# A selective-scan and expert layer in 512-token chunks: one SiLU in another stretch, paired u products, and two B·u tiles that change engines

## The reference

```python
xn = rmsnorm(layernorm(x), rms_w)
xs, res = split(xn @ W_in, 2)                 # 512 channels each
xs = silu(causal_conv4(xs) + conv_b)
dt, B, C = split(xs @ W_x, [512, 528])        # 16 states
dt = softplus(dt @ W_dt)
h_t = exp(A * dt_t) * h_{t-1} + dt_t * B_t * xs_t     # 512 channels x 16 states
y_t = sum_n h_t[:, n] * C_t[n]
x = x + layernorm(x) + (y * silu(res)) @ W_out
n2 = layernorm(x)
x = x + (silu(n2 @ w1[e]) * (n2 @ w3[e])) @ w2[e]     # expert e has tokens 512e to 512e+511
```

## Time and profile before

| | |
|---|---|
| median of 3 runs | 978.1 us (977.73 to 979.46) |
| the profiled execution, its time | 979.27 us |
| its span | 977.5 us |
| PE, DVE, POOL, ACT busy | 93%, 92%, 91%, 76% of the span |
| granted TensorE clock, mean | 0.982 |

### The profile page before, as it was taken

How to read it: one execution, slowest core, us unless ns; L and a number is a source line. 1 busy time by engine, 2 the same in 40 slices (tenths; PEclk the granted TensorE clock), 3 DMA queues, 4 the chain that set the end, 5 groups by cost and what they waited for, 6 DMA issues and landing times. The chain is left out here.

```text
span 977.5 us, 13189 instructions
## 1 busy us (share of the span) xinstructions
PE 912.5 (93%) x4204; PEld 601.2 (62%) x4204; DVE 900.1 (92%) x1000; ACT 745.8 (76%) x1356; POOL 893.5 (91%) x425
## 2 busy tenths in 40 slices
PE   6989988999999999999999999999999998677988
PEld 4555455655766566755766567655667557554777
DVE  5889899899999999999999999999999989988983
ACT  4577877888779878888879787888788876567771
POOL 1498899999999999999999999999999999998970
PEclk9998999999999999999999999999999999699999
DMA  5580145011651039111471037310580117401100
GB/s 176 227 295 22 43 164 226 1 68 59 259 202 46 23 114 353 54 68 46 182 293 40 29 102 274 144 68 0 188 331 1 47 60 264 153 22 59 52 1 22
DMA packets 43477, 116.82 MB, mean 120 GB/s; under 512 B 8592, under 2 KB 27024, under 8 KB 34192
## 3 DMA queue, kind: packets, MB, share of 16 engines
q1 hardware_dynamic: 41552, 115.94, 31.9%
q10 hardware_dynamic: 1856, 0.04, 0.1%
HBM read 110.21 MB, written 5.77 MB: 119 GB/s over the span
## 5 line engine op out<-in xcount | busy, mean ns | idle before, releaser
L701 DVE TENSOR_TENSOR_SCAN ring<-ebank,state,ring 128x512 f32<-128x512 f32 (+1 forms) x544 | 626.4, 1203 | 36.8 <-ACT ebank L864 28.7
L553 POOL TENSOR_TENSOR hc<-ring,c_all 128x1024 f32<-128x1024 f32 (+1 forms) x256 | 600.4, 2367 | 18.4 <-DVE ring L701 10.7
L864 ACT ACTIVATE ebank<-dt_,a_neg 128x512 f32<-128x512 f32 (+1 forms) x544 | 353.0, 662 | 143.0 <-DVE ring L701 139.5
L1323 PEld LDWEIGHTS ybank<-ident,hc 128*128 128x128 f32 x1920 | 221.0, 142 | 95.4 <-issue 58.0
L542 POOL TENSOR_TENSOR ring<-b_all,u 128x1024 f32<-128x1024 f32 x110 | 261.1, 2374 | 9.9 <-DVE taken L644 9.5
L1323 PE MATMUL ybank<-ident,hc 128*128 128x128 f32 x1920 | 245.2, 276 | 23.0 <-POOL hc L553 14.3
L681 DVE TENSOR_TENSOR ring<-b_all,ubank 128x1024 f32<-128x1024 f32 x144 | 172.0, 1195 | 0.0
L1248 PE MATMUL gbank<-xT,w 128*128 128x512 f32 x280 | 132.0, 603 | 7.1 <-DVE hb L811 6.8
L1248 PE MATMUL gbank<-xT,w_a 128*128 128x512 f32 x256 | 120.1, 606 | 8.0 <-DVE dt_ L669 4.4
L1248 PE MATMUL gbank<-xs,w_a 128*128 128x512 f32 x224 | 100.8, 593 | 0.7 <-ACT sres L896 0.7
L1248 PEld LDWEIGHTS gbank<-xT,w 128*128 128x128 f32 x280 | 50.2, 192 | 64.0 <-issue 46.0
(11 more groups left out here) (164 smaller groups left out, 854.9 us busy)
## 6 DMA issues: line engine op xcount, KB each, us to landing
b_all<-bc_kept SPq DMA_DIRECT2D x32, 1024.0 KB, 6.7
c_all<-bc_kept SPq DMA_DIRECT2D x32, 1024.0 KB, 8.4
w<-in_L_ffn_w_dram SPq DMA_DIRECT2D x16, 640.0 KB, 4.9
w_a<-in_L_attn_W_in_dram SPq DMA_DIRECT2D x7, 1024.0 KB, 4.8
w_a<-wc_kept SPq DMA_DIRECT2D x7, 1024.0 KB, 4.9
w2s<-in_L_ffn_w_dram SPq DMA_DIRECT2D x8, 640.0 KB, 9.3
xin<-in_L_attn_x_dram SPq DMA_DIRECT2D x9, 512.0 KB, 3.8
x<-in_L_attn_x_dram SPq DMA_DIRECT2D x7, 512.0 KB, 6.4
```

The source lines that it names most:

```text
L553: ch_ok.by(e.tensor_tensor(tile_of(hc, c, q)[:, 0:many, :], tile_of(ring, c, q)[:, 0:many, :], c_all[:, n:n + many, tok], ALU.mult))
L701: h_ok.by(e.tensor_tensor_scan(row, e_of(c, j), row, initial=all_states[:, first:first + 1], op0=ALU.mult, op1=ALU.add))
L864: e_ok.by(e.activation(e_of(c, j), dt_[:, d, tok], ACT.Exp, scale=a_neg[:, d, n0 + n:n0 + n + 1]))
L1323: last = e.matmul(ybank[:, cols(b)], hc[:, q % HC, n, cols(b)], ident[:, :], is_transpose=True, start=(k == 0 and n == 0 and b == 0), stop ...
```

## The change

Four things are done.

1. The residual SiLU of chunks 2 to 6 is made at tile 8 of the iteration that scans the chunk (in the first stretch) and not at tile 20 of the iteration before (in the second). Chunk 7's stays at tile 20 of iteration 6, and chunk 1's was in the first stretch before.
2. In chunks 1 to 6 the B·u of tile 10 goes from POOL to DVE, which makes it together with that of tile 9 after scan 8. That of tile 12 goes from DVE to POOL, which makes it after hc of tile 9.
3. u is made for two channel blocks at a time, 1024 elements: blocks 0 and 1 of the next chunk at tile 28, and blocks 2 and 3 of the scanned chunk at tile 2.
4. Iteration 0 keeps its single products for chunk 0, and makes the pair of chunk 1 at tile 28.

```diff
-    POOL_BU = (1, 4, 7, 10, 11, 14, 17, 18, 21, 22, 23, 24, 27, 29)
+    POOL_BU = (1, 4, 7, 11, 12, 14, 17, 18, 21, 22, 23, 24, 27, 29)
...
+        def steady(c):
+            return 0 < c < E - 1
...
+            def u_two(d):
+                def job(c, i):
+                    for k in (d, d + 1):
+                        wait_dt(e, c, k)
+                    xs_ok.wait(e, c)
+                    ub_ok.wait(e, c - 1, d + 2)
+                    e.tensor_tensor(u[:, d:d + 2, :], dt_[:, d:d + 2, :], xs[:, d:d + 2, :], ALU.mult).then_inc(u_ok.sem, 2)
+                return job
...
-            table = [(4, "scan", u_of(ND - 1)), (10, "back", back), (21, "next", front), (24, "front", u_of(0)),
-                     (27, "front", u_of(1)), (29, "front", u_of(2))]
...
+            table = [(2, "scan", u_two(2)), (10, "back", back), (21, "next", front), (28, "front", u_two(0))]
+            table0 = [(3, "late", u_of(1)), (7, "late", u_of(2)), (10, "late", u_of(3)), (23, "next", front), (28, "front", u_two(0))]
+            run(table, table0, [(2, "scan", u_two(2))], [], group)
...
-                if (c, q) == (E - 1, QH):
+                if (c, q) == (E - 1, QH) or (steady(c) and q == 8):
                     bu(c, q + 1)
                     bu(c, q + 2)
-                elif q + 1 < Q and q + 1 in dve_bu(c) and (c, q) != (E - 1, QH + 1):
+                elif q + 1 < Q and q + 1 in dve_bu(c) and (c, q) != (E - 1, QH + 1) and not (steady(c) and q == 9):
                     bu(c, q + 1)
...
                 xs_silus(c, i)
-                if i == 1:
-                    res_silu(c - 1, i - 1)
+                res_silu(c - 1, i - 1)
                 e.preload_act_table_set(LOG_EXP)
...
-                if has_front(i):
+                if i == E - 2:
                     res_silu(c + 2, i)
                 e.preload_act_table_set(LOG_EXP)
```

More of the change, by code:

```diff
@@ L569, in _ @@
                     bu(0, q)
-            table = [(4, "scan", u_of(ND - 1)), (10, "back", back), (21, "next", front), (24, "front", u_of(0)),
-                     (27, "front", u_of(1)), (29, "front", u_of(2))]
-            table0 = [(3, "late", u_of(1)), (7, "late", u_of(2)), (10, "late", u_of(3)), (23, "next", front),
-                      (27, "front", u_of(0)), (28, "front", u_of(1)), (29, "front", u_of(2))]
-            run(table, table0, [(4, "scan", u_of(ND - 1))], [], group)
+            table = [(2, "scan", u_two(2)), (10, "back", back), (21, "next", front), (28, "front", u_two(0))]
+            table0 = [(3, "late", u_of(1)), (7, "late", u_of(2)), (10, "late", u_of(3)), (23, "next", front), (28, "front", u_two(0))]
+            run(table, table0, [(2, "scan", u_two(2))], [], group)
         @block.vector
```

## The result

The changed kernel took **996.3 us** (median of 4 runs, 996.01 to 997.06) against 978.1 us (977.73 to 979.46): a ratio of 1.0186, 95% interval 1.0172 to 1.0201. It is slower, as forecast, but by 18.2 us where 8.5 was forecast, and outside the range of 984 to 991. The profiled execution of the changed kernel took 996.17 us at a span of 994.4 us, 16.9 above the span before.

What follows compares the result with a forecast made beforehand. The prediction took POOL to bound the steady state: a hole of 2.15 us at hc 9 makes the period 113.95 us, 1.41 above 112.54, adding 8.5 us in all to 978.1, so 986.6 us, range 984 to 991.

Steps and rivals of the forecast that it cites:

- PE would catch up: PE, 3.4 us late behind hc 12, recovers to 1.4 as its later waits vanish; at most 0.5 us per period left.
- The pairs: On POOL, four u products of 512 elements become two of 1024, saving 0.32 us per period.
- The stretch of 8.85 us and the 13.75 to hc 9: Tile 8: DVE takes 8.85 us from after scan 7 to scan 9; hc 9 starts 13.75 us after scan 7 starts.
- The stall at tile 21: DVE's stall of 1.53 us there goes with the SiLU, and POOL's wait of 0.28 us.
- So in the steady state POOL sets the pace: POOL, busy 112.11 of 112.54 us in a steady period and hardly waiting, determines the period.
- The period of 113.95: Steady period: 100.2 us of POOL's queue from hc 9 to bu 7, plus 13.75 to hc 9; 1.41 above 112.54.
- PE takes over: Rival, chance 0.07: PE's waits for DVE and ACT stay, up to 1.9 us more per period, 994.2 us.
- the forecast's ring: Chain bu 7, scan 7, scan 9, hc 9, then POOL's queue to the next bu 7; period 113.95 us.
- the part on other waits: Waits of POOL, DVE and ACT that the change touches were all taken as hidden, some by 0.6 or 1.3 us.
- The last iteration: POOL arrives 8.5 us later there, and the shift reaches DVE and the end undiminished.

Runs made afterwards that it cites:

- e8: Changed kernel with 16 identity transposes on PE, their result overwritten, just ahead of its wait for hc 12: 991.09 us, ratio 1.0128.
- e4: Changed kernel with PE making the dt product of channel block 0 ahead of the sum of tile 12: 986.80 us, ratio 1.0086.
- e5: Kernel before with only the pairs of u: 978.60 us, ratio 0.9999.
- e11: Kernel before with B·u of tile 10 moved from POOL to DVE, that of tile 12 staying on DVE: 980.18 us, ratio 1.0014.
- e1: Kernel before with only the residual SiLU moved to tile 8: 983.84 us, ratio 1.0056.
- e14: Kernel before with only B·u 10 and 12 swapped, and PE's dt product of block 0 ahead of tile 12's sum: 986.63 us, ratio 1.0079.
- e2b: Kernel before with only B·u 10 and 12 changing engines, run a second time: 997.96 us, ratio 1.0201.
- e3: Changed kernel with single products of u, as before: 998.69 us, ratio 1.0207.
- e16: Changed kernel with the SiLU put back to where it was before: 997.52 us, ratio 1.0189.

## Why the prediction was right in part and wrong in size

**The step that failed for the size** is that PE would catch up. The forecast saw PE 3.4 us late and let its waits of 1.1 and 0.8 us vanish in that lateness, with at most 0.5 us a period left over; the granted clock was no term of the sum at all. The runs show 0.87 us a period for the lateness (`e8` less `e4`) and 1.65 us for the clock (changed kernel less `e8`), 2.5 us a period in place of 0 to 0.5.

- **The pairs** (0.3 us of POOL saved per period): POOL's busy time went from 112.11 to 111.92 us in `e5`. By itself this is worth nothing in time.
- **The stretch of 8.85 us and the 13.75 to hc 9**: right to the second digit (8.85; 420.49 - 406.74 = 13.75). The stall at tile 21 went, as said.
- **"So in the steady state POOL sets the pace"**: this was read from a share of 99.6%, and it is not shown. `e5` and `e11` took 0.2 and 2.2 us of work from POOL and the period did not get shorter, so some chain that POOL's work is not in is as long. Which one is open. The traces show this much: PE is dense from hc 12's sum to its transposes at 449.87, `gated(1)` on DVE waits 0.22 us for them, scan 20 and `hidden(0)` follow, PE waits 1.14 us for that product, and PE's list then leads to the next convolution, whose evacuation by ACT leads to the exps and the scans of the next tiles 6 and 7. At its head PE waits for POOL's hc 12 in the kernel before (0.14 us), and for ACT's `hb` in `e5` (0.15 us): one chain through POOL, one past it, nearly equal. From scan 7 to the end of PE's wait for DVE it was 49.8 us and is 54.7, while the other leg went from 62.8 to 61.8.
- **The period of 113.95**: right, by its mechanism, for `e4` (113.90), where POOL's queue does set scan 7's start. That `e1` (113.85) and `e14` (113.95) come out alike is luck: in both scan 7 begins 2.3 us after the end of bu 7, so their ring is another one.
- **"PE takes over" (0.07)**: this is the rival that came true. Its lateness was worked out rightly: hc 12 was to end 27.8 us after scan 7 began, and it did. What failed is the sentence that PE's waits "vanish in its lateness, and by their kind they should". The 0.8 us for ACT's `yt` did vanish. The 1.14 us for DVE's `hb` stands unchanged, and the rows below say why: DVE's `gated(1)` waits for PE's own transposes, scan 20 and the product follow without a gap, and PE gets its bank back 3.7 us after the transposes ended, before (450.47 to 454.20) as after (457.67 to 461.40). A wait for a result that hangs on the waiting engine itself moves back with it. By its own sum the rival gave 994.2 with 1.9 us a period; the period grew by 3.88 - 1.36 = 2.5 beyond the forecast's ring.

```profile
457.07 0.60 PE L1265 MATMUL gbank<-ident,yt 128*128 128x128 f32 x4
...
457.71 0.69 DVE L726 TENSOR_TENSOR sres<-gbank,sres 128x512 f32<-128x512 f32 x1 [0.68 <-PE gbank L1265]
458.32 2.45 DVE L711 TENSOR_TENSOR_SCAN ring<-ebank,state,ring 128x512 f32<-128x512 f32 x2
460.68 1.26 DVE L821 TENSOR_TENSOR hb<-hb,gbank 128x512 f32<-128x512 f32 x2
```

- **The clock** was in no case of the forecast: 1.65 us a period, two thirds of that 2.5. In the steady periods it fell only in kernels with PE's wait of 1.97 us, though not behind each such wait; it stays at full where that wait is gone (`e4`) or filled with work (`e8`).
- **ACT's wait for `st`**: the part on other waits named the state copy, B·u 10, u 0 and the pair at tile 2, but not the `st` product that B·u 12 is put ahead of. ACT waits 1.4 us for it in the changed kernel, and DVE then 0.8 at scan 13. What this costs in time is not shown.
- **The last iteration**: POOL's shift was to reach the end undiminished. It did: from hc 9 of iteration 6 to the end 2.0 us are added, and the sum had 8.5 - 6.75 = 1.75 there (6.75 is 761.4 less 754.65).

The sum after the fact: four steady periods of + 3.88 are 15.5, the first one + 1.5, the tail + 2.0; less the 2.0 by which this execution's iteration 1 was early, that is 17.0 of the 16.9 us.

The Trainium skill (Perfetto Trace Analysis, Identifying the Most-Contended Engine) says to take the engine with the highest occupancy and to optimise that one first. For the steady period that was POOL, and the measurements differ: relieving it bought nothing (`e5`, `e11`). Where three engines are busy for 97 to 99.6% of a period, the share does not tell which chain of waits closes the period.

## What to carry to other kernels

Before a product is moved to an engine with "room", follow every consumer of what it now delays to a third engine, and measure there how many us the result was early: here PE already waited 0.14 us for hc 12, had nothing to spare, and 2.3 us of new work went ahead of it on POOL. When an engine is late, ask of each of its later waits whether the awaited result depends on that engine itself; only waits that don't can absorb the lateness. Filling a wait of PE with matmuls whose result is thrown away (`e8`) gave back 1.65 us a period. To find out whether a nearly full engine alone sets the pace, take work from it in one run rather than read its share, and see to it that the work does not land on another nearly full engine, as it did in `e11`.

## What the runs showed of the hardware

PE's wait of 1.95 to 1.99 us for hc 12 occurs six times in each of four profiles (the changed kernel, `e2b`, `e3`, `e16`). Within 1.2 us of the end of 19 of these 24 waits the granted clock went to 0.50 for 3.4 us, and the eight 512-column products behind the wait took 4.24 to 5.29 us; at the other 5 it stayed at 1.00, and they took 3.60 us. Length alone does not decide it, and what does is open: the same wait of the same kernel did both. In steady periods without that wait the clock never fell, though PE waited up to 1.4 us (for DVE, in `e4`). In `e8`, with 16 small matmuls and a wait of 0.23 us in the same place, the clock stayed at 1.00.

The Trainium skill (TensorE: Matmul & The Clock Gate, Part 1: The HAM clock gate) says that the clock is 2.4 GHz for an engine that has been busy and 1.2 GHz for one that has been idle. The trace agrees on the two levels; a wait of 1.97 us in an otherwise dense list was enough to bring the lower one in 19 of 24 cases.
